# First attention layer of a four-layer kernel: probabilities turned by VectorE in 32x32 blocks and moved by DMA, outputs scaled by GpSimd

## The reference

```python
wc = weights of x and of the context side by side        # K = 2 x 256 input rows
q, k, v = wc @ concat(x, u)                               # per batch and head: 64 x 512
s = (q + r_w_bias)^T k / 8                                # 512 x 512
p = softmax(s, over k)
o = v p^T                                                 # 64 x 512
att = x + Wo concat(o over heads)                         # 256 x 512
x1 = column and row norm of att + bo                      # goes to the second layer
```

## Time and profile before

| | us |
|---|---|
| median of 3 runs | 3532.03 |
| lowest and highest | 3530.91, 3532.55 |
| span of the profiled execution | 3531.3 |
| TensorE busy | 3298.1 |
| VectorE busy | 2377.8 |
| ScalarE busy | 1780.9 |
| GpSimd busy | 202.5 |

### The profile page before, as it was taken

How to read it: one execution, slowest core, us unless ns; L and a number is a source line. 1 busy time by engine, 2 the same in 40 slices (tenths; PEclk the granted TensorE clock), 3 DMA queues, 4 the chain that set the end, 5 groups by cost and what they waited for, 6 DMA issues and landing times. The chain is left out here.

```text
span 3531.3 us, 55048 instructions
## 1 busy us (share of the span) xinstructions
PE 3298.1 (93%) x21408; PEld 2528.1 (72%) x21408; DVE 2377.8 (67%) x3781; ACT 1780.9 (50%) x4249; POOL 202.5 (6%) x319
## 2 busy tenths in 40 slices
PE   8999999999999997789999998769999999699998
PEld 6777888787777785556666655457887788488885
DVE  6666666666665665599999999537777878542213
ACT  5554444444454443446565554327777777532222
POOL 0000000000000000000000000001111111000000
PEclk9999999999999999989999999779999999899999
DMA  6322212221122211544454544130011110210004
GB/s 216 127 106 101 108 72 81 96 111 72 72 96 90 79 72 59 162 111 115 110 117 110 120 112 111 38 108 13 25 43 62 46 43 31 93 48 24 24 12 162
DMA packets 95697, 300.42 MB, mean 85 GB/s; under 512 B 20144, under 2 KB 28336, under 8 KB 70992
## 3 DMA queue, kind: packets, MB, share of 16 engines
q1 hardware_dynamic: 64960, 186.60, 18.2%
q0 software_dynamic: 12544, 79.70, 6.4%
q10 hardware_dynamic: 17936, 30.59, 2.4%
HBM read 233.95 MB, written 62.91 MB: 84 GB/s over the span
## 5 line engine op out<-in xcount | busy, mean ns | idle before, releaser
L537 ACT ACTIVATE l_prob<-l_bank,l_nmax 128x512 f32<-128x512 f32 x512 | 344.8, 686 | 276.9 <-DVE l_nmax L679 276.9
L679 DVE TENSOR_REDUCE l_nmax<-l_bank 128x1 f32<-128x512 f32 x512 | 317.3, 681 | 71.4 <-PE l_bank L409 71.3
L375 PE MATMUL l_bank<-l_x_hi,l_w_hi 128*128 128x256 f32 x1024 | 297.6, 291 | 11.3 <-DVE l_x_lo L779 11.3
L702 DVE COPY l_probT<-l_bank 128x512 f32<-128x512 f32 x256 | 173.6, 689 | 175.3 <-PE l_bank L423 174.6
L375 PE MATMUL l_bank<-l_x_hi,l_w_lo 128*128 128x256 f32 x1024 | 290.4, 284 | 0.0
L375 PE MATMUL l_bank<-l_x_lo,l_w_hi 128*128 128x256 f32 x1024 | 290.3, 284 | 0.0
L1744 DVE TENSOR_TENSOR_SCAN l_kv<-l_wx,l_kv 128x2056 f32<-128x2056 f32 x64 | 283.8, 4434 | 3.1 <-DVE l_sxc L1865 1.5
L2318 ACT ACTIVATE l2a_sc<-l2a_sc,l2a_nmax 128x256 f32<-128x256 f32 x512 | 254.8, 508 | 41.1 <-DVE l2a_nmax L2434 41.1
L423 PE MATMUL l_bank<-l_ident,l_prob 128*128 128x128 f32 x2048 | 247.9, 275 | 10.6 <-DVE l_k_lo L695 6.3
L423 PEld LDWEIGHTS l_bank<-l_ident,l_prob 128*128 128x128 f32 x2048 | 225.8, 141 | 24.3 <-DVE l_k_lo L695 16.2
L445 PE MATMUL l_bank<-l_probT,l_v 128*64 128x512 f32 x1024 | 233.8, 598 | 0.0
(11 more groups left out here) (351 smaller groups left out, 8177.3 us busy)
## 6 DMA issues: line engine op xcount, KB each, us to landing
l_vb<-vd SPq DMA_DIRECT2D x64, 1024.0 KB
l_w_hi<-kept_w_hi POOLq DMA_DIRECT2D x24, 1024.0 KB, 8.3
l_w_lo<-kept_w_lo POOLq DMA_DIRECT2D x24, 1024.0 KB, 10.3
l_wv_hi<-kept_wv_hi POOLq DMA_DIRECT2D x12, 1024.0 KB, 5.1
l_wv_lo<-kept_wv_lo POOLq DMA_DIRECT2D x12, 1024.0 KB, 7.1
kept_w_hi<-l_w_hi SPq DMA_DIRECT2D x8, 1024.0 KB, 8.7
kept_w_lo<-l_w_lo SPq DMA_DIRECT2D x8, 1024.0 KB, 11.2
l2a_x<-x SPq DMA_DIRECT2D x16, 512.0 KB, 3.6
```

The source lines that it names most:

```text
L375: mm = pe.matmul(s.ap[:, c * ROWS:(c + 1) * ROWS], a[:, kt, c, g, :], b[:, kt, c * ROWS:(c + 1) * ROWS], start=m == 0, stop=m == 3 * KT - 1)
L537: act.activation(prob[h][:, it, :], s.ap[:, :], ACT.Exp, bias=nmax[:, n % 2, it, h:h + 1], accum_out=rsum[:, n % 2, it, h:h + 1]).then_inc ...
L679: dve.tensor_reduce(nmax[:, n % 2, it, h:h + 1], s.ap[:, :], AX.X, ALU.max, negate=True).then_inc(max_ready, 1)
L702: dve.tensor_copy(probT[0][:, j, :], s.ap[:, :]).then_inc(s.drained, 1)
```

## The change

The 32 transposes of a step on TensorE go. VectorE transposes the probabilities in place, each 32x32 block by itself, in four instructions a step (`turns`, 128x1024). What is left, to carry block column r of partition group g to partition group r, is done by DMA: 16 transfers of 32 partitions x 2 KB for each half of a step (two row blocks, both heads), nine of them issued by SP and seven by GpSimd (`move`). `prob` and `probT` are rings of three halves. A transfer into a ring place waits until the values were weighed with what stood there (`full` of the o tile), exponentials into one wait until it was moved (`half_moved`). The exponentials write in blocks of 32 columns.

TensorE's order in step n becomes: scores 0 and 1, queries of n+1, keys of n+1, scores 2 and 3, sums of n-1, output projection of n-2, weighing of n-1, values of n+1. The weighing has 16 products of 256 columns, whose moving operand has runs of 32 elements. ScalarE now makes the hi part of the queries and copies the weighed outputs to `oT`, GpSimd multiplies `oT` by `rT` in place (`scale_outputs`), ScalarE rounds it to `oT_hi`, VectorE subtracts for `oT_lo`. To make room, `wraw` shares the buffer of the norm (`first["anx"]`), and `wvraw` that of `xraw` and, for the first group, `probT`. SP issues its loads and stores between its moves, GpSimd its weight loads after the moves of a step. No product or function is left out.

```diff
+    SQ, Q = 32, 4
+    RING = 3
+    NB = COLS // SQ
     SCALE = 1.0 / 8.0
     HALF = TURNS * HP * LANES
     QUADS = HP // 2
+    MOVES = [(g, r) for g in range(Q) for r in range(Q)]
+    BY_SP = 9
     H2 = range(2)
     NORM = HALF - 14
+    X1 = NORM + 5
...
-    for n in range(-1, HALF + 1):
-        if n > 0:
+    for n in range(-1, HALF + 2):
+        if n + 1 < HALF:
+            order += [f"q{n + 1}"]
+        if n + 1 < HALF:
+            order += [f"k{n + 1}"]
+        order += {BIAS: ["cb"], CENTRE: ["nc_0", "nc_1"], VAR: ["nv"], SPREAD: ["nr"]}.get(n, [])
+        if 0 < n <= HALF:
+            order += [f"r{n - 1}"]
+        if n > 1:
+            order += [f"w{n - 2}_0", f"w{n - 2}_1"]
+        if 0 < n <= HALF:
             order += [f"o{n - 1}"]
         if n + 1 < HALF:
-            order += [f"q{n + 1}"]
-        if n > 0:
-            order += [f"w{n - 1}_0", f"w{n - 1}_1"]
-        if n + 1 < HALF:
-            order += [f"k{n + 1}"] + ([f"v{n + 1}_0", f"v{n + 1}_1"] if where(n + 1)[1] % 2 == 0 else [])
-        if 0 <= n < HALF:
-            order += [f"t{n}_{j}{h}" for j in range(IT) for h in H2] + [f"r{n}"]
-            order += {BIAS: ["cb"], CENTRE: ["nc_0", "nc_1"], VAR: ["nv"], SPREAD: ["nr"]}.get(n, [])
+            order += [f"v{n + 1}_0", f"v{n + 1}_1"] if where(n + 1)[1] % 2 == 0 else []
...
-        wraw, wvraw = ph.sb("wraw", [P, KT, 2, 2, P]), ph.sb("wvraw", [P, KT, 2, 2, P])
+        wraw = first["anx"][:, :, :, :].rearrange("p a r n -> p (a r n)").rearrange("p (k c g o) -> p k c g o", k=KT, c=2, g=2)
...
-        prob = [ph.sb(f"prob{h}", [P, IT, COLS]) for h in H2]
-        probT = [ph.sb(f"probT{h}", [P, IT, COLS]) for h in H2]
+        prob = [ph.sb(f"prob{i}", [P, NB, 2, 2, SQ]) for i in range(RING)]
+        probT = [ph.sb(f"probT{i}", [P, Q, IT, 2, 2, SQ]) for i in range(RING)]
...
+        wo_raw = probT[2][:, :, :, :, :, :].rearrange("p b t i h s -> p (b t i h s)").rearrange("p (q n) -> p q n", q=HP)
+        wvraw0 = probT[1][:, :, :, :, :, :].rearrange("p b t i h s -> p (b t i h s)").rearrange("p (k c i o) -> p k c i o", k=KT, c=2, i=2)
+        wvraw = xraw[:, :, :].rearrange("p k n -> p (k n)").rearrange("p (k c i o) -> p k c i o", k=KT, c=2, i=2)
...
+        def half_moved(eng, i):
+
+            eng.wait_ge(moved_sp[i % RING], 16 * BY_SP * (i // RING + 1))
+            eng.wait_ge(moved_pool[i % RING], 16 * (len(MOVES) - BY_SP) * (i // RING + 1))
+
+        def move(eng, n, f, pieces, moved):
+
+            i = 2 * n + f
+            eng.wait_ge(turned, IT * n + 2 * f + 2)
+            if i >= RING:
+                full(eng, S[f"o{(i - RING) // 2}"])
+            elif i == 1:
+                eng.wait_ge(wv_lo_ready, 1)
+            elif i == 2:
+                eng.wait_ge(wo_lo_ready, 1)
+            for g, r in pieces:
+                eng.dma_start(probT[i % RING][r * SQ:(r + 1) * SQ, g, :, :, :, :],
+                              prob[i % RING][g * SQ:(g + 1) * SQ, r * IT:(r + 1) * IT, :, :, :]).then_inc(moved[i % RING], 16)
...
+                split_weights(0)
+                for n in range(HALF):
+                    bp, pair, l = where(n)
+                    move(sp, n, 0, MOVES[:BY_SP], moved_sp)
+                    move(sp, n, 1, MOVES[:BY_SP], moved_sp)
+                    if bp == 0 and l == 0 and pair + 1 < HP:
+                        split_weights(pair + 1)
+                    if pair == (0 if bp else HP - 3) and l == 1 and bp + 1 < TURNS:
+                        sp.wait_ge(wv_lo_ready, QUADS)
+                        load_x(bp + 1, 0)
+                    if pair == HP - 1 and l == 0 and bp + 1 < TURNS:
+                        load_x(bp + 1, 1)
+                    if pair == 0 and bp:
                         store_acc(bp - 1, l)
                         load_acc(bp, l)
...
+                def spread_sums(n):
                     pool.wait_ge(rinv_ready, n + 1)
                     if n:
                         full(pool, S[f"r{n - 1}"])
                     pool.tensor_copy(rows[:, :, :, :], rinv[:, n % 2, :, :].unsqueeze(3).to_broadcast([P, IT, 2, D])).then_inc(rows_ready, 1)
+
+                def scale_outputs(n):
+                    drained(pool, S[f"o{n}"])
+                    drained(pool, S[f"r{n}"])
+                    pool.tensor_tensor(oT[:, :], oT[:, :], rT[:, :], ALU.mult).then_inc(scaled, 1)
+
+                for n in range(HALF + 2):
+                    if 0 < n <= HALF:
+                        spread_sums(n - 1)
+                    if n > 1:
+                        scale_outputs(n - 2)
+                    if 0 < n <= HALF:
+                        move(pool, n - 1, 1, MOVES[BY_SP:], moved_pool)
+                    if n >= HALF:
+                        continue
+                    move(pool, n, 0, MOVES[BY_SP:], moved_pool)
...
-                    for j in range(IT):
-                        for h in H2:
-                            own = slice(D * h, D * h + D)
-                            drained(pe, S[f"t{n}_{j}{h}"])
-                            mm = pe.matmul(s.ap[own, :], v[l][:, pair % 2, j, own], probT[h][:, j, :], start=j == 0, stop=j == IT - 1)
+                    for f in range(2):
+                        half_moved(pe, 2 * n + f)
+                        half = probT[(2 * n + f) % RING][:, :, :, :, :, :].rearrange("p g t i h s -> p i g t h s")
+                        for j in range(IT):
+                            for h in H2:
+                                own = slice(D * h, D * h + D)
+                                mm = pe.matmul(s.ap[own, f * ROWS:(f + 1) * ROWS], v[l][:, pair % 2, j, own], half[:, :, :, j, h, :],
+                                               start=j == 0, stop=j == IT - 1)
...
                     scores(n, (0, 1))
-                    if n:
-                        weigh_values(n - 1)
-                    scores(n, (2, 3))
                     if n + 1 < HALF:
                         project(n + 1, "q")
-                    if n:
-                        project_out(n - 1)
-                    if n + 1 < HALF:
                         project(n + 1, "k")
-                        project_v(n + 1)
-                    turn_probs(n)
-                    turn_sums(n)
+                    scores(n, (2, 3))
                     if n == BIAS:
                         bias_rows()
                     if n == CENTRE:
...
                         column_variances()
                     if n == SPREAD:
                         spread_deviations()
+                    if n:
+                        turn_sums(n - 1)
+                    if n > 1:
+                        project_out(n - 2)
+                    if n:
+                        weigh_values(n - 1)
+                    if n + 1 < HALF:
+                        project_v(n + 1)
+                turn_sums(HALF - 1)
+                project_out(HALF - 2)
...
+                    i = 2 * n + its[0] // 2
+                    if i >= RING:
+                        half_moved(act, i - RING)
                     for it in its:
                         for h in H2:
                             s = S[f"s{n}_{it}{h}"]
                             act.wait_ge(max_ready, 2 * IT * n + 2 * it + h + 1)
-                            act.activation(prob[h][:, it, :], s.ap[:, :], ACT.Exp, bias=nmax[:, n % 2, it, h:h + 1],
+                            act.activation(prob[i % RING][:, :, it % 2, h, :].rearrange("p (q t) s -> p t q s", q=Q),
+                                           s.ap[:, :].rearrange("p (t q s) -> p t q s", t=IT, q=Q), ACT.Exp, bias=nmax[:, n % 2, it, h:h + 1],
                                            accum_out=rsum[:, n % 2, it, h:h + 1]).then_inc(s.drained, 1)
...
+                def queries(n):
+                    bp, pair, l = where(n)
+                    s = S[f"q{n}"]
+                    full(act, s)
+                    act.activation(q_hi[l][:, :], s.ap[:, :], ACT.Identity, bias=rb[:, pair:pair + 1]).then_inc(q_hi_ready, 1)
 
                 def sums(n):
                     s = S[f"r{n}"]
                     full(act, s)
+                    act.wait_ge(scaled, n)
+                    act.activation(rT[:, :], s.ap[:, :], ACT.Copy).then_inc(s.drained, 1)
+
+                def weighed(n):
+                    s = S[f"o{n}"]
+                    full(act, s)
                     if n:
-                        drained(act, S[f"o{n - 1}"])
-                    act.activation(rT[:, :], s.ap[:, :], ACT.Copy).then_inc(s.drained, 1)
+                        act.wait_ge(oT_ready, n)
+                    act.activation(oT[:, :], s.ap[:, :], ACT.Copy).then_inc(s.drained, 1)
+
+                def outputs(n):
+                    act.wait_ge(scaled, n + 1)
+                    if n:
+                        full(act, S[f"w{n - 1}_{RT - 1}"])
+                    act.activation(oT_hi[:, :], oT[:, :], ACT.Copy).then_inc(oT_hi_ready, 1)
...
+                    if n > 1:
+                        weighed(n - 2)
```

(59 more changed lines are left out.)

86 lines of the change are left out of this document (31 added, 55 removed).

## The result

The changed kernel takes 3453.88 us (median of four runs, 3452.93 to 3459.09) beside 3531.47 for the kernel before on the same chip: a ratio of 0.978, 95% interval 0.977 to 0.980. It is 2.2% faster, 78 us. The prediction had the direction right and named 208 us.

The account below looks back on a forecast made before the run. TensorE was taken as the bound: 3531.3 - 239 (transposes) + 8 (splits) + 15 (queue) + 8 (end) = 3323, for a median of 3324 us. The range was 3275 to 3480 us.

Parts of the forecast that it names:

- Transposes, -239: TensorE, first layer: removing 32 transposes a step saves 3.73 us in the mean, 239 us over 64 steps.
- The weighing, 0: TensorE's weighing of values: 16 products of 256 columns with runs of 32 cost nothing more than the 3.59 us before.
- Rival 4: TensorE's weighing: short runs of 32 halve its rate, +3.6 us a step, about 3550 us; chance 0.04.
- VectorE, GpSimd, Sync: Their work per step, 13.9, 10.4 and 8.5 us, fits under TensorE's 14.55 us short step.
- Rivals 1 and 2: GpSimd bounds at 1.23 us a move, 3460 us, chance 0.09; VectorE bounds at 2.5 us a transpose, 3430 us, chance 0.08.
- The DMA engines: Moves take 5.5 to 8.2 us a step, existing traffic 5.5; together 11 to 13.7 of 17.4, so it fits.
- The queue, +15: GpSimd's DMA queue: moves behind four weight loads come 0 to 3 us late in 12 steps, charged 15 us.
- this cover: The 2.5 us to spare between half 1's moves landing (t + 8.4) and TensorE's weighing needing them (t + 10.9).
- Splits in turn 0, +8: VectorE, first 16 steps: splitting weights adds 2.3 us in three steps of four, charged 8 us in all.
- The end, +8: End of the first layer: 22 us after the last exponential instead of 19.0, and step 63 lacks covering projections; charged 8 us.
- Rival 5: Every step: moves land so late that waits give back just what the transposes cost, 3532 us; chance 0.04.

Follow-up runs that it names:

- e1: Changed kernel with GpSimd issuing the weight loads of turns 1 to 3 before the moves of half 0 of their step: 3471.39 us, 0.984.
- e2: Changed kernel with the same weight loads issued from ScalarE's own DMA queue instead of GpSimd's: 3468.09 us, 0.983.
- e6: Changed kernel with GpSimd issuing its moves of half 1 before it scales the outputs: 3459.76 us, 0.979.
- e3: Changed kernel with fifteen sixteenths of each weight load of turns 1 to 3 left out, same number of issues, result incomplete: 3376.11 us, 0.957.
- e9: Changed kernel with the value weights issued a step later, so no step gets more than 2 MB of loads: 3408.74 us, 0.965.
- e4: Changed kernel with the next accumulator's load issued one step after the old one's store, not right behind it: 3432.02 us, 0.972.
- e10: Changed kernel with SP storing and loading the value weights of turn 0 a step earlier: 3439.25 us, 0.974.
- e8: Changed kernel with two groups of norm operations put at the end of their steps on TensorE and in its bank order: 3442.42 us, 0.975.
- e7: Changed kernel with half of each move's bytes left out from the fourth half on, same number of transfers, result incomplete: 3389.25 us, 0.959.

## Why the prediction was wrong in size

The 75 us that the layer won, by the two profiles, are the sum of three parts:

- **The work of TensorE at full clock.** An undisturbed step takes 17.69 us, where it took 84.57 / 4 = 21.14: 3.46 x 64 = 221 us less.
- **Its idle time.** 125.4 instead of 34.1 us: 91 more.
- **Its clock.** At full clock 1365.2 - 221 = 1144 us would be busy; the window shows 1198.6: 54 more. This is a remainder, and most of it is clock: in the trace of the changed kernel the granted clock is 0.50 for 130 us of the layer, and TensorE is busy in 99 of them, half of which is lost; before these were 11 and 9 us. That makes 45 of the 54.

-221 + 91 + 54 = -76. Now by the terms of the prediction's own sum:

- **Transposes, -239.** Measured -221. The mechanism was right. A step with values takes 20.66 for 20.28, one without 14.71 for 14.55.
- **The weighing, 0.** Right: 632.59 - 628.99 = 3.60 us beside 3.59 before. Rival 4 is out.
- **VectorE, GpSimd, Sync.** Near: 1.228 us a transpose, 0.501 an issue, 1.28 a scaling; only Sync's issues took more, 0.59 in the median for 0.47. Rivals 1 and 2 are out; GpSimd is busy 10.8 us in the step from 617.88, VectorE 12.4.
- **The DMA engines.** I worked out 11 to 13.7 us of 17.4 and concluded that it fits. The mean share of 0.72 to 0.76 bears out the numbers and not the conclusion. The moves of a step take 8.0 us, within my 5.5 to 8.2. But of each four steps one has 14.7 us for its moves and for most of four loads. I had put the 5.5 us a step of what was there already into the mean, though the earlier trace rows showed that they come together.
- **The queue, +15. This is the term that failed**, in mechanism and in size. I took the delay as one of order, moves behind loads in GpSimd's queue, 0 to 3 us late in 12 steps. Another order or another queue brings no gain (e1, e2, e6). The engines are full and SP's moves come late as well (8.0 us). The steps were the right ones, and there were 12 of them, but they cost 68 us and not 15: waits of 2.4 to 3.7 us in turns 1 and 2, and the clock behind them. 55 of the 68 go without the loads' bytes (e3) and 50 once no step gets 4 MB (e9). The prediction did say that this cover could go, and charged about a fifth of its price.
- **The turn's start, not in the sum.** The store that SP waits for was in the kernel before as well, where no move stood behind it. The prediction gave Sync its nine issues without a wait, and did not look at what blocks its queue. TensorE waited 7.6 us there at the start of turns 1 and 2, and a later load gives 22 us (e4).
- **Splits in turn 0, +8.** The 16 steps of turn 0 take 329 us, 46 over 16 x 17.69; before they were 12 over, so 34 and not 8. Of these, 10 lie in step 14, behind the first reloads, and are in the 68 above. e10 takes 9 us out of the turn; what the splits themselves cost was not taken apart. The order of the norm, +11, was not in the sum (e8).
- **The end, +8.** From the last exponential (1297.73) to 1324.22 it is 26.5 us where I had 22, and the first step starts 3.8 us later.
- **The clock, not in the sum.** Before, TensorE had no wait above 1.1 us between 37 and 1379 us, and the clock stayed at 1.00. Now its granted clock falls to half in or behind a longer wait, as from 650.0 to 653.5, so a wait of 3.50 us cost a step 5.5 (20.17 for 14.71). No run changed the clock alone. In e3 and in most of e9 it went back to 1.00 with the waits, so their gains hold both.

Rival 5, that waits give all of it back, came nearest in kind: they give back two thirds. Its place was wrong. It is not in every step, and GpSimd's cycle is not what sets it.

## What to carry to other kernels

When traffic is added to DMA engines, draw up the bytes for each step, with the size and issue time of every burst, and compare the fullest step with its own length; a mean share of 0.75 may hide a step that does not fit, and one of 0.83 may fit (e9). If it doesn't, delay the transfer that is needed last, and look for waits in every queue through which new urgent transfers go. Price a wait of TensorE with the stretch at half clock that may follow it.

## What the runs showed of the hardware

- TensorE's granted clock was 1.00 in the layer before from 37 to 1381 us, with a TensorE that hardly idled, and 0.50 for short stretches at its start and end, beside waits of 4.63 and 1.96 us. In the changed kernel it is 0.50 for 23 stretches of about 3.4 or 6.8 us and for the last 11 us. Nearly all begin in or right behind a wait of 2.1 us or more (3.50 us at 649.16, 7.56 at 435.55). The length of the wait alone doesn't settle it: one began 1.6 us behind a wait of 1.36 us (76.28), one at 1293.02 behind none above 1 us, and behind waits of 1.54 us (151.10) and 2.83 us (1304.26) the clock stayed at 1.00. In the stretch from 650.0 to 653.5 the DMA share is 0.03, so transfers aren't what slows TensorE there.
- Transfers of 64 KB from SBUF to SBUF, 32 partitions by 2 KB, 32 a step on two queues, ran at some 260 GB/s when busy. Their cost went with the bytes: with half of them, at the same count, the share of the engines in a step fell from 0.42 to 0.22 (e7), and the kernel was 65 us faster.
- GpSimd issued such a transfer in 0.50 us, like one of 1 MB (0.56): the 1.23 us of the nearest row for a store did not carry over.
- VectorE's transpose in 32x32 blocks took 1.228 us for 128x1024 float32, the same as the subtraction of that size.
